# A layer norm's root and rows on GpSimd, and low parts by subtraction on VectorE, in a linear-attention and mixture-of-experts kernel

## The chip, the cores and the metric

One core of a Trainium2 chip runs the whole program. The metric is device microseconds (us) from start to end of one execution, as the median of several runs. The core has TensorE (matmuls; PE in the profile), VectorE (DVE), ScalarE (ACT), GpSimd (POOL) and SyncE (SP, which here only issues DMAs). GpSimd can't read the matmul banks (PSUM); the others can.

## The reference

```python
x = L0_attn_x                                    # (8, 512, 256), fp32
xn = (x - mean(x)) / sqrt(var(x) + 1e-5)         # over the last axis
out = x + attention(xn) + ffn(xn)

# attention: 16 heads of 16, 128 random features
q, k, v = split(xn @ W_qkv.T)
q_p = elu(q @ proj) + 1;  k_p = elu(k @ proj) + 1          # per head, 16 -> 128
kv = k_p.T @ v;  z = 1 / (q_p @ k_p.sum(tokens) + 1e-8)
attention = ((q_p @ kv) * z) @ W_out.T + b_out

# ffn: 8 experts, each token to its 2 best
logits = xn @ Wr + br; weights = softmax of the two largest logits, 0 elsewhere
ffn = sum over experts e of weights[:, e] * (gelu(xn @ W1[e] + b1[e]) @ W2[e] + b2[e])
```

## The kernel before

The program has two parts. The attention part works through 8 batches of 512 tokens and lasts until about 300 us; the expert part works through tiles of up to 384 tokens and is not touched by the change.

Matmuls run in fp32r, a rounded form of fp32. To keep fp32's accuracy, each operand is held as two parts: a high part (the value rounded to fp32r) and a low part (value minus high part, rounded). A product is then three matmuls (`mm3`, lines L527 to L529). The low part of queries, keys and head outputs is made in this way: ScalarE copies a PSUM bank into the high tile (`qk_hi`, L1038, into kdh or qdh; `at_hi`, L1067, into ath), TensorE multiplies that tile by the negated identity `minus` and adds it onto the same bank (`qk_rest`, L555; `heads_rest`, L647), so that the bank holds the low part, and ScalarE copies it out (`qk_lo`, L1043, into kdl or qdl; `at_lo`, L1071, into atl). For the tokens themselves (`tokens_lo`, L1395, into xTl) VectorE subtracts the high tile from the bank, one instruction of 128x512, and TensorE has no part in it.

A batch b is one call of `iteration(b)` on each of TensorE, ScalarE and VectorE, with 32 units u. Each unit makes the features of one bank: TensorE computes F (L590 in units 0 to 15, L596 in 16 to 31), ScalarE takes the exponential (`exp`, L1063, into a ring of four), VectorE combines both (`features`, L1468, into kp or qp). TensorE's unit u waits until VectorE has done the features of unit u - 4. Between the units, in an order written out by hand for each engine (`if u == ...`), lies the rest: attention of batch b - 1, and queries, keys, values, router and layer norm of the batches b + 1 and b + 2. Order within an engine is strict; semaphores tie the engines together, also where a bank is used again. In the order of TensorE: `tokens_T` of the next batch in unit 2 (it needs xn), `kv` in units 10, 11, 17 and 19 (L605), `qk_rest` of bank 0 in unit 11, of bank 1 in unit 18, of bank 2 in unit 23 and of bank 3 in unit 30, `to_heads` (L640) in units 20 and 27, which write banks that the low parts of keys and queries must have left, `heads_rest` in units 21 and 28, `state_T` (L613) at unit 26.

The layer norm of batch b + 2 is made on VectorE: `norm_stats` (4 instructions, L1350) in units 16 and 17, `norm_var` (4 small ones, L1355) in unit 18, nine small steps of 128x4 (`norm_step`, L1363 to L1379: variance plus eps, a bit-trick first guess of 1/sqrt, and two refinements) in units 19 to 29, and `norm_rows` (4 instructions of 128x256, L1386, which write xn) in unit 0 of the next iteration. `load_x` on SP refills xin once `norm_rows` has read it.

GpSimd, in each iteration b, scatters the 512 token rows to the experts' lists (`send`, 8 indirect DMAs, L1866, each waiting for a unit of TensorE: 0, 2, 4 to 14), adds the output bias to the residual (`add_bias`, L1853) and copies the next batch's xn into rows (`copy_rows`, L1860). SP issues the DMAs that stack the high and low parts into Sk and Sq (`stack_k`, `stack_q`, 12 DMAs each, L350), and the loads of x.

Of the kernel before, what the change touches and what calls it, by code (L numbers as in the profile page):

```python
# [19 lines left out]
I32 = mybir.dt.int32  # L20
# [33 lines left out]
C_END = C_OFF + E * TT  # L54


def constants():

    import numpy as np
    c = np.zeros((P, C_END), np.float32)  # L60
    p = np.arange(P)
    c[:, C_ID:C_ID + P] = np.eye(P)
    c[:, C_TRI:C_TRI + P] = p[:, None] < p[None, :]
    c[:, C_SLOT:C_SLOT + NT * E] = np.tile(np.arange(E) * CAP - SKIP, NT)
    c[:, C_TOK:C_TOK + NB * NT] = (NT * p[:, None, None] + NTOK * np.arange(NB)[:, None] + np.arange(NT)).reshape(P, -1)
    c[:, C_PAD:C_PAD + SUB] = p[:, None] + P * np.arange(SUB) + TOKENS
    c[:, C_EPS] = 1e-8 * DOWN * (p % 32 >= HD)
    c[:, C_T:C_T + TT] = np.arange(TT)
    c[:, C_LIM:C_LIM + E] = np.arange(E) * CAP - 2 * P
    c[:, C_OFF:C_OFF + E * TT] = (np.arange(E)[:, None] * CAP + T * np.arange(TT)).reshape(-1)  # L70
    return c


def build(nc, x, w_in, proj, w_out, b_out, experts, b1, b2, br, consts, out):
# [170 lines left out]
    xn_first = sem("xn_first")  # L245
    xT_full = sem("xT_full")
# [74 lines left out]
    NORM_STEPS, CUBE = 9, 0.375  # L321
    STEPS_AT = {19: (0, 1), 21: (2,), 23: (3, 4), 24: (5,), 25: (6,), 26: (7,), 29: (8,)}
# [48 lines left out]
    def _(sp):  # L371
# [66 lines left out]
        with sp.Fori(1, NB - 2) as b:  # L438
            load_x(b + 2)
            stack_k(b + 1)  # L440
            stack_q(b + 1)
            store_o(b - 1)
            load_xres(b)
        stack_k(NB - 1)
        stack_q(NB - 1)
        store_o(NB - 3)
        load_xres(NB - 2)
# [76 lines left out]
    def _(pe):  # L524
# [145 lines left out]
        def iteration(b, first=False):  # L670
# [4 lines left out]
            for u in range(32):  # L675
# [32 lines left out]
                if u == 11:  # L708
                    kv(b, 1)
                    qk_rest(b + 1, 0)  # L710
# [10 lines left out]
                if u == 18:  # L721
                    qk_rest(b + 1, 1)
# [291 lines left out]
    def _(act):  # L1014
# [25 lines left out]
        def qk_lo(b, i):  # L1040

            act.wait_ge(qkr_full, 4 * b + i + 1)
            A((kdl, qdl)[i // 2][:, i % 2, :], QK_BANK[i][:, :], ACT.Copy).then_inc(qkl_rdy, 1)  # L1043
# [25 lines left out]
        def at_lo(b, g):  # L1069
            act.wait_ge(atr_full, 2 * b + g + 1)  # L1070
            A(atl[:, g, :], AT_BANK[g][:, :], ACT.Copy).then_inc(atl_rdy, 1)  # L1071
# [27 lines left out]
        def iteration(b, first=False):  # L1099
            for u in range(32):  # L1100
# [15 lines left out]
                if u == 11:  # L1116
                    qk_lo(b + 1, 0)
                if u == 15:
                    qk_hi(b + 1, 1)
                if u == 19:  # L1120
                    qk_lo(b + 1, 1)
                    v_copy(b + 1, 0)
                if u == 20:
                    copy_kv(b)
                    if not first:
                        at_hi(b - 1, 0)
                    qk_hi(b + 1, 2)
                    if not first:
                        at_lo(b - 1, 0)
                if u == 22:  # L1130
                    qk_lo(b + 1, 2)
# [164 lines left out]
    def _(dve):  # L1296
# [61 lines left out]
        def norm_step(b, i):  # L1358
# [5 lines left out]
            elif i == 1:  # L1364
                link(V.tensor_scalar(seed.bitcast(I32), var[:, :].bitcast(I32), -0.5, float(0x5F3759DF), ALU.mult, ALU.add))
# [157 lines left out]
        def iteration(b, first=False, ahead=True):  # L1523
            for u in range(32):
                if u == 0 and not first:
                    norm_rows(b + 1, 0, 4)
# [18 lines left out]
                if ahead:  # L1545
                    if u == 16:
                        norm_stats(b + 2, 0, 2)
                    if u == 17:
                        norm_stats(b + 2, 2, 4)
                        join()  # L1550
                    if u == 18:
                        norm_var(b + 2)
                    for i in STEPS_AT.get(u, ()):
                        norm_step(b + 2, i)
# [172 lines left out]
        iteration(0, first=True)  # L1727
        batch_steps = chain[1] - before
        with dve.Fori(1, NB - 2) as b:
            chain[:] = before + b * batch_steps, 0  # L1730
            iteration(b)
# [103 lines left out]
    def _(pool):  # L1835
# [9 lines left out]
        pool.reg_mov(turn, 33)  # L1845
# [16 lines left out]
        def send(b):  # L1862
# [17 lines left out]
            for n in range(NT):  # L1880
                for r in range(2):
# [5 lines left out]
                    send_block(n, r, sent)  # L1887

        pool.wait_ge(qkh_rdy, 2)
        copy_rows(0)  # L1890
        send(0)
        copy_rows(1)
        with pool.Fori(1, NB - 1) as b:
            send(b)
            add_bias(b - 1)
            copy_rows(b + 1)
        def split_weights(c):
# [87 lines left out]
```

## Time and profile before

| | |
|---|---|
| time, median of 3 runs (lowest to highest) | 700.12 us (699.78 to 701.21) |
| the profiled execution's own time | 700.86 us |
| its span, first to last instruction | 698.7 us |
| busy: PE, DVE, ACT, POOL | 682.9, 504.1, 475.3, 227.9 us |
| mean granted TensorE clock | 0.996 of full speed |

The durations below come from the profiled execution. A row of the timeline reads: start in us from the span's start, duration in us, engine, line, operation, output<-inputs, shape, xN for N neighbours merged in one row; in square brackets the time the engine stood idle before the row, and what ended it. Because instructions of one engine overlap a little at their edges, the cost of one on its engine is the distance from its start to the start of the next, not its duration. A row of a stretch (A:B) gives its length and then, for PE, PEld, DVE, ACT and POOL, the busy time and the number of instructions, then the granted clock, the DMA engines' busy share and GB/s.

### The profile page before, as it was taken

Reading aid. Unit: us, or ns where it says so; the run is one execution under the profiler, and the core shown is the slowest. Engines: PE = TensorE matmul, PEld = TensorE weight load, DVE = VectorE, ACT = ScalarE, POOL = GpSimd, SP = SyncE. Lnnn points to the kernel's source line nnn. Section 1 sums busy time; section 2 is a strip of 40 time slices with the busy share of each in tenths; the row PEclk is TensorE's granted clock in tenths of the full one; section 3 lists DMA queues with packets and bytes.
Section 4 is the critical chain, followed back from the end, with each engine's and each line's share of the span. In section 5 each row is a group of like instructions: output and inputs, shape, how many; then the busy total and the mean of one; then the engine's idle time right before and its main releaser. Section 6 shows DMA issues by size and latency. Waiting matters only on the chain.

```text
span 698.7 us, 17362 instructions
## 1 busy us (share of the span) xinstructions
PE 682.9 (98%) x5503; PEld 603.3 (86%) x5504; DVE 504.1 (72%) x1246; ACT 475.3 (68%) x875; POOL 227.9 (33%) x169
## 2 busy tenths in 40 slices
PE   8899999999999998999999999999999999999996
PEld 4666777777777776589999999999999999999996
DVE  8798888888888878748577675556777545577544
ACT  5687969696969696776557775447775444577553
POOL 2053232323232324643232532225233222322422
PEclk9999999999999999999999999999999999999999
DMA  8856474747474647765455663336556333454531
GB/s 266 200 182 170 108 228 106 228 106 228 106 228 106 198 106 223 224 189 142 100 98 118 145 167 46 46 47 106 178 71 167 48 52 53 81 131 107 69 48 23
DMA packets 87205, 91.65 MB, mean 131 GB/s; under 512 B 60049, under 2 KB 73361, under 8 KB 84897
## 3 DMA queue, kind: packets, MB, share of 16 engines
q1 hardware_dynamic: 71426, 59.36, 33.9%
q0 software_dynamic: 13872, 18.75, 15.2%
q10 hardware_dynamic: 1872, 13.11, 5.1%
q8 instruction: 17, 0.28, 0.2%
q14 instruction: 18, 0.15, 0.1%
HBM read 39.32 MB, written 26.67 MB: 94 GB/s over the span
## 4 chain that ended last, share of the span: by engine, by line
PE 82%; DVE 6%; issue 4%; ACT 2%; POOL 2%; DMA 2%; SPq 1%; POOLq 0%; DVEq 0%
PE F L527 9%; PE F L528 9%; PE F L529 9%; PE WK L527 5%; PE F L596 5%; PE WK L529 4%; PE WK L528 4%; PE NUM L527 4%; PE NUM L529 4%; PE NUM L528 4%; PE DEN L605 4%; PE DEN L527 4%; PE DEN L529 4%; PE DEN L528 4%; PE F L590 3%
## 5 line engine op out<-in xcount | busy, mean ns | idle before, releaser
L1932 POOL DMA_INDIRECT out<-ysb,icur x75 | 121.0, 1613 | 270.6 <-DVE ysb L1763 241.0
L1218 ACT ACTIVATE h<-F,b1c 128x384 f32<-128x384 f32 x200 | 112.2, 575 | 140.0 <-PE F L529 131.2
L1740 DVE TENSOR_TENSOR hl<-h,hh 128x768 fp32r<-128x768 f32 x100 | 96.1, 962 | 111.6 <-ACT hh L1222 111.6
L1063 ACT ACTIVATE e_ring<-F 128x512 f32<-128x512 f32 x256 | 145.7, 621 | 38.5 <-PE F L590 35.0
L527 PE MATMUL F<-gxh,wh 128*128 128x384 f32 (+1 forms) x400 | 128.6, 321 | 0.4 <-DVE wl L1641 0.4
L528 PE MATMUL F<-gxl,wh 128*128 128x384 f32 (+1 forms) x400 | 128.0, 320 | 0.0
L529 PE MATMUL F<-gxh,wl 128*128 128x384 f32 (+1 forms) x400 | 128.0, 320 | 0.0
L1866 POOL DMA_INDIRECT xg<-rows,slots x64 | 63.2, 988 | 174.0 <-PE F L590 158.8
L1468 DVE SCALAR_TENSOR_TENSOR kp<-F,e_ring 128x512 f32<-128x512 f32 x128 | 82.7, 680 | 13.2 <-PE DEN L605 6.2
L1468 DVE SCALAR_TENSOR_TENSOR qp<-F,e_ring 128x512 f32<-128x512 f32 x128 | 85.2, 683 | 8.5 <-ACT e_ring L1063 7.0
L1222 ACT ACTIVATE hh<-h 128x768 fp32r<-128x768 f32 x100 | 84.6, 846 | 3.3
L527 PEld LDWEIGHTS F<-gxh,wh 128*128 128x128 f32 x400 | 75.6, 189 | 2.5 <-issue 2.5
L528 PEld LDWEIGHTS F<-gxl,wh 128*128 128x128 f32 x400 | 75.6, 189 | 0.0
L529 PEld LDWEIGHTS F<-gxh,wl 128*128 128x128 f32 x400 | 75.6, 189 | 0.0
L590 PEld LDWEIGHTS F<-stacked_proj,Sk 97*128 97x128 f32 x256 | 38.0, 192 | 26.0 <-issue 13.9
L527 PE MATMUL DEN<-wh,hh 128*128 128x256 f32 x200 | 56.7, 283 | 0.6 <-issue 0.6
L527 PE MATMUL NUM<-wh,hh 128*128 128x256 f32 x200 | 56.6, 283 | 0.2 <-DVE hl L1740 0.2
L528 PE MATMUL DEN<-wl,hh 128*128 128x256 f32 x200 | 56.6, 283 | 0.0
L529 PE MATMUL DEN<-wh,hl 128*128 128x256 f32 x200 | 56.6, 283 | 0.0
L529 PE MATMUL NUM<-wh,hl 128*128 128x256 f32 x200 | 56.5, 283 | 0.0
L528 PE MATMUL NUM<-wl,hh 128*128 128x256 f32 x200 | 56.5, 282 | 0.0
L596 PE MATMUL F<-Sq,stacked_proj 97*128 97x512 f32 x128 | 52.3, 450 | 0.3 <-DVE qp L1468 0.3
(261 smaller groups left out, 1552.6 us busy)
## 6 DMA issues: line engine op xcount, KB each, us to landing
wraw<-experts ACTq DMA_DIRECT2D x12, 1024.0 KB, 6.2
gblk<-xg SPq DMA_DIRECT2D x100, 96.0 KB
Sk<-kdh SPq DMA_DIRECT2D x64, 128.0 KB, 2.3
Sq<-qdh SPq DMA_DIRECT2D x64, 128.0 KB
xin<-x SPq DMA_DIRECT2D x8, 512.0 KB, 5.5
Sk<-kdl SPq DMA_DIRECT2D x32, 128.0 KB, 2.4
Sq<-qdl SPq DMA_DIRECT2D x32, 128.0 KB
xres<-x SPq DMA_DIRECT2D x8, 512.0 KB
```

The lines of the kernel that those rows point to most:

```text
L527: nc.tensor.matmul(dst, wh_, mh_, start=first, stop=False)
L528: nc.tensor.matmul(dst, wh_, ml_, start=False, stop=False)
L529: return nc.tensor.matmul(dst, wl_, mh_, start=False, stop=last)
L590: last = nc.tensor.matmul(F[u % 4][:, s * D:(s + 1) * D], Sk[0:SROWS, place_of(pr), n * P:(n + 1) * P], stacked_proj[0:SROWS, 2 * pr:2 * p ...
L596: last = nc.tensor.matmul(F[h % 4][:, :], stacked_proj[0:SROWS, h, :], Sq[0:SROWS, place_of(h // 2), :], start=True, stop=True)
L1063: A(e_ring[:, u % 4, :], F[u % 4][:, :], ACT.Exp, bias=EXP_BIAS, scale=1.0 / DOWN).then_inc(exp_done, 1)
L1218: A(h32[:, m, :], F[m % 4][:, 0:T], ACT.Gelu, bias=b1c[:, w, m:m + 1]).then_inc(gelu, 1)
L1222: A(hh[:, 2 * q:2 * q + 2, :], h32[:, 2 * q:2 * q + 2, :], ACT.Copy).then_inc(hh_rdy, 1)
L1468: V.scalar_tensor_tensor(dst, F[u % 4][:, :], DOWN, e_ring[:, u % 4, :], ALU.max, ALU.min).then_inc(feat, 1)
L1740: V.tensor_tensor(hl[:, 2 * q:2 * q + 2, :], h32[:, 2 * q:2 * q + 2, :], f32(hh[:, 2 * q:2 * q + 2, :]), ALU.subtract).then_inc(hl_rdy, 1)
L1866: pool.indirect_dma_start(xg, bass.IndirectOffsetOnAxis(slots[:, k:k + 1], 0), rows[:, n, :], None, bounds_check=last_row, oob_is_err=Fals ...
L1932: pool.indirect_dma_start(out, bass.IndirectOffsetOnAxis(icur[:, s, :], 0), ysb[:, s, :], None, bounds_check=last_token, compute_op=ALU.ad ...
```

## The change

- `norm_stats`, `norm_var` and the first two norm steps move from units 16 to 19 to units 0, 1 and 2 of `iteration(b)` for b from 2 on; iterations 0 and 1 have them in units 16 to 18 (`late=True`). Iteration 6 has none in either kernel.
- The other seven steps leave VectorE for batches 2 to 7. GpSimd does them as eleven instructions of 128x4 (`norm_root`), each waiting for the one before by a semaphore. They stand behind the third of the eight scatters (for b from 2 on), or behind all of them (b = 0), or behind the bias (b = 1).
- `norm_rows` of batches 2 to 7 leaves VectorE. GpSimd does it behind `add_bias` and `copy_rows`, some 13 units earlier than VectorE did.
- `qk_rest` of banks 0, 1 and 2 goes, in iterations 0 to 6, and `heads_rest` of bank 0 in iterations 1 to 6; with them go ScalarE's copies of the low parts. VectorE subtracts instead (`qk_low` in units 8, 17 and 24; in iteration 0 unit 12 for the first; `heads_low` in unit 21). Bank 3, head bank 1, and the whole start and final iteration stay as they were.
- On SP, `load_x` stands between `stack_k` and `stack_q` instead of ahead of both, one batch further ahead.

```diff
+        def qk_low(b, i):
+            dve.wait_ge(qkh_rdy, 4 * b + i + 1)
+            high, low = ((kdh, kdl), (qdh, qdl))[i // 2]
+            V.tensor_tensor(low[:, i % 2, :], QK_BANK[i][:, :], f32(high[:, i % 2, :]), ALU.subtract).then_inc(qkl_rdy, 1)
+        def heads_low(b):
+            dve.wait_ge(ath_rdy, 2 * b + 1)
+            V.tensor_tensor(atl[:, 0, :], AT_BANK[0][:, :], f32(ath[:, 0, :]), ALU.subtract).then_inc(atl_rdy, 1)
...
 # TensorE, iteration
                 if u == 11:
                     kv(b, 1)
-                    qk_rest(b + 1, 0)
-                if u == 18:
-                    qk_rest(b + 1, 1)
                 if u == 21:
-                    if not first:
-                        heads_rest(b - 1, 0)
                     v_logits(b + 1, 1)
                 if u == 23:
-                    qk_rest(b + 1, 2)
...
 # VectorE
-        def iteration(b, first=False, ahead=True):
+        def iteration(b, first=False, ahead=True, late=False):
             for u in range(32):
-                if u == 0 and not first:
-                    norm_rows(b + 1, 0, 4)
+                if ahead and u == (16 if late else 0):
+                    norm_stats(b + 2, 0, 2)
+                if ahead and u == (17 if late else 1):
+                    norm_stats(b + 2, 2, 4)
+                    join()
+                if ahead and u == (18 if late else 2):
+                    norm_var(b + 2)
+                    for i in range(SEED_STEPS):
+                        norm_step(b + 2, i)
...
+                if u == (12 if first else 8):
+                    qk_low(b + 1, 0)
+                if u == 17:
+                    qk_low(b + 1, 1)
+                if u == 21 and not first:
+                    heads_low(b - 1)
+                if u == 24:
+                    qk_low(b + 1, 2)
...
 # GpSimd
+        def norm_rows(b, i):
+            pool.wait_ge(root_step, ROOT_STEPS * i + 11)
+            pool.wait_ge(rows_rdy, b)
+            pool.wait_ge(xT_full, KT * b)
+            for n in range(NT):
+                last = nc.gpsimd.tensor_scalar(xn[:, n, :], xin[:, n, :], mv[:, n, 0:1], rs[:, 1, n:n + 1], ALU.subtract, ALU.mult)
+            last.then_inc(xn_rdy, 1)
...
         send(0)
+        norm_root(2, 0)
         copy_rows(1)
-        with pool.Fori(1, NB - 1) as b:
-            send(b)
+        norm_rows(2, 0)
+        send(1)
+        add_bias(0)
+        norm_root(3, 1)
+        copy_rows(2)
+        norm_rows(3, 1)
+        with pool.Fori(2, NB - 2) as b:
+            send(b, root=b)
             add_bias(b - 1)
             copy_rows(b + 1)
+            norm_rows(b + 2, b)
```

## Rows read from the trace of the kernel before

**Rows 1.** Busy time of two stretches: iterations 0 and 2.
```profile
22.40:57.44 35.04, 32.00 (x288) 22.16 (x286) 30.04 (x104) 27.32 (x60) 9.14 (x9) 0.95 0.67 182
92.47:127.51 35.04, 34.92 (x332) 26.44 (x328) 31.00 (x90) 28.66 (x61) 11.24 (x11) 1.00 0.61 166
```

**Rows 2.** Timeline of PE, iteration 2 and the start of iteration 3.
```profile
92.47 0.50 PE L590 MATMUL F<-stacked_proj,Sk 97*128 97x256 f32 x2
...
102.07 0.50 PE L555 MATMUL NUM<-kdh,minus 128*128 128x512 f32 x1
102.41 0.65 PE L590 MATMUL F<-stacked_proj,Sk 97*128 97x256 f32 x4
...
109.03 0.60 PE L640 MATMUL WK<-cst,at 128*128 128x128 f32 x4
...
112.57 0.40 PE L555 MATMUL WK<-qdh,minus 128*128 128x512 f32 x1
112.81 0.28 PE L527 MATMUL DEN<-WTh,xTh 128*128 128x264 f32 x1
...
113.54 1.02 PE L596 MATMUL F<-Sq,stacked_proj 97*128 97x512 f32 x3
114.39 0.60 PE L613 MATMUL WK<-cst,kv_sb 128*128 128x128 f32 x4
...
127.51 0.50 PE L590 MATMUL F<-stacked_proj,Sk 97*128 97x256 f32 x2
```

**Rows 3.** Groups by line, DVE, 92.47 to 127.51: busy us, mean ns | idle.
```profile
L1350 DVE BATCH_NORM_STATS2 stats<-xin 128x6 f32<-128x256 f32 x4 | 1.5, 414 | 0.0
L1386 DVE TENSOR_SCALAR xn<-xin,mv,rs 128x256 f32<-128x256 f32 x4 | 1.4, 407 | 0.0
L1395 DVE TENSOR_TENSOR xTl<-WK,xTh 128x512 fp32r<-128x512 f32 x1 | 0.7, 691 | 0.9 <-issue 0.9
L1371 DVE SCALAR_TENSOR_TENSOR rtmp<-rtmp 128x4 f32<-128x4 f32 x1 | 0.2, 162 | 0.0
```

**Rows 4.** Timeline of DVE, iteration 2: its three idle places and one feature.
```profile
94.08 0.69 DVE L1395 TENSOR_TENSOR xTl<-WK,xTh 128x512 fp32r<-128x512 f32 x1 [0.85 <-issue]
94.69 0.68 DVE L1395 TENSOR_TENSOR xTl<-NUM,xTh 128x512 fp32r<-128x512 f32 x1
...
100.77 0.69 DVE L1468 SCALAR_TENSOR_TENSOR kp<-F,e_ring 128x512 f32<-128x512 f32 x1 [0.86 <-PE DEN L605]
...
109.30 0.69 DVE L1468 SCALAR_TENSOR_TENSOR qp<-F,e_ring 128x512 f32<-128x512 f32 x1
...
112.72 1.29 DVE L1468 SCALAR_TENSOR_TENSOR qp<-F,e_ring 128x512 f32<-128x512 f32 x2 [0.30 <-ACT e_ring L1063]
```

**Rows 5.** Timeline of DVE, iteration 0.
```profile
34.78 3.07 DVE L1468 SCALAR_TENSOR_TENSOR kp<-F,e_ring 128x512 f32<-128x512 f32 x5
37.77 0.68 DVE L1344 TENSOR_TENSOR WOl<-wout,WOh 128x512 fp32r<-128x512 f32 x1
```

**Rows 6.** Timeline of POOL, iteration 2.
```profile
98.31 0.97 POOL L1866 DMA_INDIRECT xg<-rows,slots  x1 [2.20 <-PE F L590]
...
106.56 2.41 POOL L1853 TENSOR_TENSOR xres<-xres,bo_bc 128x1024 f32<-128x1024 f32 x1
108.88 1.06 POOL L1860 COPY rows<-xn 128x1024 f32<-128x1024 f32 x1
```

**Rows 7.** DMA issues, 92 to 128 us: KB each, us to landing.
```profile
xin<-x SPq DMA_DIRECT2D x1, 512.0 KB, 7.0
```

**Rows 8.** Timeline of the start: a POOL copy, a DVE instruction beside it.
```profile
14.54 2.29 DVE L1339 SCALAR_TENSOR_TENSOR stacked_proj<-praw,phi 33x2048 fp32r<-33x2048 f32 x1
15.04 2.69 POOL L1860 COPY rows<-xn 128x1024 f32<-128x1024 f32 x1 [12.96 <-ACT kdh L1038]
```

**Rows 9.** Groups by line, POOL, 0 to 3 us: the smallest with a shape.
```profile
L1849 POOL MEMSET rows<- 128x32 f32 x1 | 0.1, 123 | 0.0
```

**Rows 10.** Timeline of SP, iteration 2: the last four stacking DMAs of the keys.
```profile
111.52 2.50 SPq L350 DMA_DIRECT2D Sk<-kdl  x4
```

More of the change, by code:

```diff
@@ L53 @@
 C_T, C_LIM, C_OFF = 324, 336, 344
-C_END = C_OFF + E * TT
+C_ROOT = C_OFF + E * TT
+C_END = C_ROOT + 4
+CUBE = 0.375
 def constants():
@@ L245, in build @@
     xn_first = sem("xn_first")
+    seed_rdy = sem("seed_rdy")
+    root_step = sem("root_step")
+    root_rdy = sem("root_rdy")
     xT_full = sem("xT_full")
@@ L437, in _ @@
         stack_q(1)
-        with sp.Fori(1, NB - 2) as b:
-            load_x(b + 2)
+        load_x(3)
+        with sp.Fori(1, NB - 3) as b:
+            stack_k(b + 1)
+            load_x(b + 3)
+            stack_q(b + 1)
+            store_o(b - 1)
+            load_xres(b)
+        for b in (NB - 3, NB - 2):
             stack_k(b + 1)
@@ L1040, in qk_lo @@
         def qk_lo(b, i):
-            act.wait_ge(qkr_full, 4 * b + i + 1)
+            act.wait_ge(qkr_full, i + 1 if isinstance(b, int) and b == 0 else 4 + b)
             A((kdl, qdl)[i // 2][:, i % 2, :], QK_BANK[i][:, :], ACT.Copy).then_inc(qkl_rdy, 1)
@@ L1364, in norm_step @@
             elif i == 1:
-                link(V.tensor_scalar(seed.bitcast(I32), var[:, :].bitcast(I32), -0.5, float(0x5F3759DF), ALU.mult, ALU.add))
+                guess = V.tensor_scalar(seed.bitcast(I32), var[:, :].bitcast(I32), -0.5, float(0x5F3759DF), ALU.mult, ALU.add)
+                if isinstance(b, int) and b < 2:
+                    link(guess)
+                else:
+                    guess.then_inc(seed_rdy, 1)
             elif i == 2:
@@ L1726, in _ @@
         before = chain[1] + ROUTE_STEPS
-        iteration(0, first=True)
+        iteration(0, first=True, late=True)
         batch_steps = chain[1] - before
-        with dve.Fori(1, NB - 2) as b:
+        iteration(1, late=True)
+        with dve.Fori(2, NB - 2) as b:
             chain[:] = before + b * batch_steps, 0
@@ L1860, in copy_rows, with norm_root, constant @@
             nc.gpsimd.tensor_copy(rows[:, :, 0:D], xn[:, :, :]).then_inc(rows_rdy, 1)
-        def send(b):
+        def norm_root(b, i):
+            G = nc.gpsimd
+            seed, cubic, root = rs[:, 1, :], rs[:, 0, :], rs[:, 1, :]
+            def constant(k):
+                return cst[:, C_ROOT + k:C_ROOT + k + 1].to_broadcast([P, NT])
+            pool.wait_ge(seed_rdy, i + 1)
+            G.tensor_tensor(rtmp[:, 0, :], seed, seed, ALU.mult).then_inc(root_step, 1)
+            pool.wait_ge(root_step, ROOT_STEPS * i + 1)
+            G.tensor_tensor(rtmp[:, 1, :], rtmp[:, 0, :], var[:, :], ALU.mult).then_inc(root_step, 1)
+            pool.wait_ge(root_step, ROOT_STEPS * i + 2)
+            G.tensor_tensor(rtmp[:, 0, :], rtmp[:, 1, :], constant(0), ALU.add).then_inc(root_step, 1)
+            pool.wait_ge(root_step, ROOT_STEPS * i + 3)
+            G.tensor_tensor(rtmp[:, 0, :], rtmp[:, 0, :], rtmp[:, 1, :], ALU.mult).then_inc(root_step, 1)
+            pool.wait_ge(root_step, ROOT_STEPS * i + 4)
+            G.tensor_tensor(rtmp[:, 0, :], rtmp[:, 0, :], constant(1), ALU.add).then_inc(root_step, 1)
+            pool.wait_ge(root_step, ROOT_STEPS * i + 5)
+            G.tensor_tensor(cubic, rtmp[:, 0, :], seed, ALU.mult).then_inc(root_step, 1)
+            pool.wait_ge(root_step, ROOT_STEPS * i + 6)
+            G.tensor_tensor(rtmp[:, 0, :], cubic, cubic, ALU.mult).then_inc(root_step, 1)
+            pool.wait_ge(root_step, ROOT_STEPS * i + 7)
+            G.tensor_tensor(rtmp[:, 1, :], rtmp[:, 0, :], var[:, :], ALU.mult).then_inc(root_step, 1)
+            pool.wait_ge(root_step, ROOT_STEPS * i + 8)
+            G.tensor_tensor(rtmp[:, 0, :], rtmp[:, 1, :], constant(2), ALU.mult).then_inc(root_step, 1)
+            pool.wait_ge(root_step, ROOT_STEPS * i + 9)
+            G.tensor_tensor(rtmp[:, 0, :], rtmp[:, 0, :], constant(3), ALU.add).then_inc(root_step, 1)
+            pool.wait_ge(root_step, ROOT_STEPS * i + 10)
+            G.tensor_tensor(root, rtmp[:, 0, :], cubic, ALU.mult).then_inc(root_step, 1)
@@ L1887, in send @@
                     send_block(n, r, sent)
+                    if root is not None and (n, r) == (1, 0):
+                        norm_root(b + 2, root)
         pool.wait_ge(qkh_rdy, 2)
```

35 lines of the change are left out of this document (10 added, 25 removed).

## The prediction

> **What bounds the kernel now.** I read the busy time by stretches first, because a share over the whole span says nothing of one stage. In iteration 2 TensorE is busy 34.92 of 35.04 us, VectorE 31.00, ScalarE 28.66, GpSimd 11.24, at the full clock [rows 1]. A busy TensorE can still be held up a little, so the second view is its timeline: unit 2 starts at 92.47 and again at 127.51, a period of 35.04 us [rows 2], and the starts within it follow each other at the pace of the moving columns (0.24 us for 512) nearly everywhere. Iterations 1 to 6 have that period. TensorE is the bound, and VectorE is next, with 4.0 us of air per iteration. Its own timeline tells where the air is: 0.85 us before it takes low parts of the tokens, 0.86 us in unit 8 (it waits for a `kv` to free kp), 0.30 us in unit 21, and smaller bits at the end [rows 4]. Between units 9 and 21 it has next to none. Iteration 0 is different: TensorE is busy only 32.00 of 35.04 us, VectorE 30.04 [rows 1], and from 34.78 on VectorE's features follow one another without a gap, 0.60 us each [rows 5]; there VectorE leads.
>
> **What TensorE loses.** One removed matmul costs the distance to the next start: 112.57 to 112.81, 0.24 us; 102.07 to 102.41 is 0.34, but 0.10 of it is the price of following a `kv`, which the next matmul will pay instead [rows 2]. Three in each of iterations 0 to 6 and one more in each of 1 to 6 are 27 matmuls, 27 x 0.233 = 6.3 us, or 0.93 per full iteration (0.233 is the finer value of the same distance). All lie on the engine that sets the pace, if the others follow.
>
> **What VectorE gains and loses.** A low part of 128x512 from a bank costs 94.69 - 94.08 = 0.61 us [rows 4]. Four are 2.44 us. It loses `norm_rows`, four of 407 ns that overlap to 1.3 us, and seven steps of about 162 ns [rows 3], 1.1 us with their gaps. So a full iteration's work stays within 0.1 us of what it was: 31.0 of now 34.1 us. Only the place of each can hurt.
>
> **Iterations 2 to 6, in place.** Units 0 and 1: four `norm_stats` (414 ns each [rows 3], 1.3 us) stand where `norm_rows` stood. Unit 2: `norm_var` and two steps, six small instructions, at most 6 x 0.16 = 0.97, with overlap some 0.7 us, in the 0.85 us of air ahead of 94.08 [rows 4]. Unit 8: `qk_low` of bank 0, 0.61 us in the 0.86 us ahead of 100.77 [rows 4]; without this cover it would delay features 8 and on, and TensorE with them. Units 16 to 26: 1.3 us of statistics, 0.7 us of `norm_var` with two steps and five other steps (0.8 us) go, three low parts (1.83 us) come, so VectorE comes out 1.0 us ahead, against the 0.93 us by which TensorE wants to be early. This is tight in one place: the three units from 113.54 on take 0.85 us until 114.39 instead of 3 x 0.233 plus 0.10, for the third needs the features that end at 112.72 + 1.29 = 114.01 [rows 2, 4]. They depend on the exponential of unit 22, which TensorE starts 0.70 us earlier, and on one that ScalarE no longer holds up by copies. `to_heads` in unit 20 writes the bank that the second low part must leave: TensorE comes there at 109.03 - 0.47 = 108.56 [rows 2]; VectorE, free of statistics, is through with that low part at about 108.2. I take 0.07 us per iteration as lost to such brushes: 5 x (0.93 - 0.07) = -4.3 us.
>
> **Iteration 1.** Here the statistics, `norm_var` and two steps stay in units 16 to 18, and what VectorE saves lies in unit 0, ahead of a wait for TensorE at unit 8, so it is no help later. The second low part comes where the feature of 109.30 begins (a batch earlier, 74.26): 0.24 us earlier by the removed matmul and the exponentials behind it, so it ends at 109.30 - 0.24 + 0.61 = 109.67, and `to_heads`, now at 109.03, starts 0.64 us late [rows 2, 4]. Then `heads_low` adds 0.61 more on VectorE, one step goes (-0.15), its 0.30 us of air is used up, and the features that TensorE needs at 114.01 end some 0.4 us later than now. After that TensorE works without a gap. Iteration 1: +0.4 instead of -0.93.
>
> **Iteration 0.** The first low part stands in unit 12, behind features 9 to 11 of the gapless stretch of [rows 5]: +0.61; the second in unit 17: +1.22; of the steps only 0.45 us are gone by unit 22, and the third low part comes in unit 24. TensorE has little slack there: with four banks in the ring, and features 0.60 us apart, unit 17 can't start before feature 13 ends, and the row of five, features 9 to 13, ends at 34.78 + 3.07 = 37.85, 0.1 us ahead of unit 17's start at 37.97. I find the features that unit 26 needs 0.6 to 0.7 us later than now, with nothing behind it to make that up. Iteration 0: +0.6 instead of -0.70.
>
> **GpSimd.** It has 35.0 - 11.2 = 23.8 us free. No trace row shows one of its 128x4 instructions. From below: the 128x32 memset of 123 ns [rows 9], and a wait on the one before, put at nothing: 11 x 0.123 = 1.4 us. From above: the 128x1024 copy of 1.06 us [rows 6], 11.7 us. I take 2.5 us, 0.1 more for each than the smallest row, for the wait. They begin after the third scatter (98.31 - 2.20 = 96.1) and end by 98.7; the fourth scatter was to start at 98.31, and 2.20 us of idle stand before it [rows 6]. So the scatters end when they did, and the bias (2.41) and the copy too: 109.9. `norm_rows` of 4 x 256 elements lies between a copy of 1024 (1.06) and a two-input instruction of 1024 (2.41) [rows 6]; I take 1.7. xn is ready at 111.6, while TensorE asks for it at 127.5. The Trainium skill, GPSIMD Engine Reference, 4.1, calls one-input work on GpSimd about as fast as VectorE; by that page it would be an estimated 1.1 us, and the sum the same.
>
> **SP.** `load_x` now waits behind the last stacking DMA, issued until 111.52 + 2.50 = 114.0 [rows 10], so xn is not what it waits for. It takes 7.0 us to land [rows 7]: 121. VectorE reads it from 125.6 - 0.9 on. Air: 3.7 us. What it no longer stands ahead of (the keys' stacking) can only come sooner. Iteration 1 is closer: its seeds come in unit 18, 77.4 with the delays above; then root 2.5, copy 1.06, rows 1.7: 82.7, landing 89.7, and the statistics of iteration 2 are due at 90.6 + 1.0 = 91.6. With 11.7 us for a root they would be 7 us late.
>
> **A shared port.** A GpSimd copy that takes 1.06 us elsewhere took 2.69 at 15.04, beside a VectorE instruction with both inputs in SBUF; it ended at 17.73, 0.90 us behind that one's end at 16.83 [rows 6, 8]. The Trainium skill, SBUF — State Buffer, Who interferes with whom, has the rule: VectorE with two SBUF inputs and a reading GpSimd instruction exclude one another for a whole instruction, and one that reads a bank and one tile does not. By that rule the trace agrees. Here the low parts read a bank, so they are free. Only VectorE's small router instructions read two tiles, and in iteration 1 `norm_rows` falls on them (82 us): up to 1.7 us on VectorE, with 2 us of TensorE's slack there; I put 0 in the sum and 1 us in the range.
>
> **Sum.** -4.3 + 0.4 + 0.6 = -3.3 us on the profiled execution's 700.86 (span 698.7, 2.16 us around it): 697.6. The runs' median of 700.12 lies 0.74 lower than that execution: **696.8 us**. The final iteration, start and expert part move along unchanged.
>
> **Rivals.**
> - *TensorE pays in full.* VectorE keeps up in iterations 0 and 1 too: -6.3, 693.8 us. For it: TensorE's waits are single tenths. Against: the gapless features. Chance 0.13.
> - *VectorE becomes the pace in all iterations.* If a low part hits a place without air each time (0.61 twice ahead of unit 26, as in iteration 1), each full iteration gives nothing: 5 x 0 + 1.0 = +1.0, 701.1 us; half of that, 699. Against: the removed 1.3 us of statistics in just that stretch. Chance 0.15.
> - *GpSimd is late.* From a root of about 10 us on, x lands after VectorE asks for it. Statistics sit ahead of features 0 and 1, so TensorE stops. If each of the 11 cost as much as a scatter, 0.97 us [rows 6] and a gap of some 0.3, the root were 14.2 us: some 4.2 us late in iterations 3 to 5, and 9 in iteration 2: +21.6, 718 us. Decides at 0.9 us per instruction, and between 0.4 and 0.9 only iteration 2 suffers (1 to 4 us, so 698 to 701). Against: 123 ns for a memset. Chance 0.07 for late in all, 0.05 for iteration 2 alone.
> - My forecast with its own range of 695.6 to 698.4: 0.60.
>
> **Range and chances.** Below, the first rival (0.13) is left out all but its near side; above, the late GpSimd. 694.6 to 700.4. A difference under 0.2% (1.4 us) can't be told from none. Faster: 0.60 + 0.13 + a few of the others = 0.75. Same: 0.15. Slower: 0.10.
>
> **What the profile after would show.** Right: 21 matmuls of L555 and 6 of L647 fewer, the period from unit 2 to unit 2 34.1 to 34.2 us in iterations 2 to 6 but 35 or more in 0 and 1, idle of TensorE in iteration 1 in front of `to_heads` released by VectorE's kdl, xTl still preceded by air, the root's instructions on GpSimd 0.2 to 0.3 us apart, and xn done before 113. Wrong: 34.1 also in iteration 1; a wait for x on VectorE in unit 0; features, not matmuls, ending TensorE's waits in iterations 2 to 6; GpSimd instructions of 128x4 near 1 us.

## The result, and the profile after

The changed kernel takes 695.18 us (median of 4 runs, 694.57 to 695.41), the kernel before, measured beside it, 700.07 (4 runs, 699.78 to 701.21). The ratio is 0.9924, with a 95% interval of 0.9912 to 0.9936: faster by 0.76%, where 0.47% (696.8 us) was forecast. The profiled execution took 695.41 us, its span is 693.6.

The head of the page first: the span, then busy time and number of instructions by engine.

```profile
span 693.6 us, 17240 instructions
PE 675.2 (97%) x5476; PEld 596.9 (86%) x5477; DVE 507.4 (73%) x1207; ACT 464.2 (67%) x848; POOL 270.4 (39%) x259
```

TensorE has 27 matmuls fewer (5503 before, 5476 now) and its busy time fell by 7.7 us. Some 2 us of that are not the matmuls' (before's profiled execution had a stretch at half clock, and the changed kernel with such a stretch is busy 677.3 us, see iteration 0 below). The span fell by 5.1. GpSimd is busy 42 us more, and under 0.3 us of that shows in the time.

Busy time by stretches, of iterations 1 and 2, from unit 0 to unit 0 (the columns are those of [rows 1]):

```profile
53.60:89.86 36.26, 34.31 (x328) 25.72 (x324) 32.60 (x90) 27.68 (x59) 20.56 (x27) 1.00 0.59 155
89.86:123.82 33.96, 33.84 (x328) 25.72 (x324) 31.40 (x84) 26.92 (x57) 18.42 (x25) 1.00 0.64 172
```

In iteration 2 TensorE is idle for 0.12 us of 33.96: it is still the bound, and the period has shrunk with its work. In iteration 1 it is idle for 1.95 us, and the period of 36.26 is longer than before. The unit-0 starts of both kernels (the first matmul of the unit on TensorE's timeline) give the time of each iteration:

| us | start of unit 0 | it. 0 | it. 1 | it. 2 to 5, each | it. 6 |
|---|---|---|---|---|---|
| before | 20.58 | 33.42 | 35.61 | 35.03 | 35.01 |
| after | 20.54 | 33.06 | 36.26 | 33.97 | 34.07 |
| difference | -0.04 | -0.36 | +0.65 | -1.07 | -0.94 |

The differences add up to -4.96 us, and what follows iteration 6 is 0.15 us shorter. So the gain comes from iterations 2 to 6 alone (-5.2 us), and iteration 1 takes 0.65 back.

The prediction counts from unit 2 to unit 2. By that count iteration 0 takes 33.85 us before and 33.78 after, iteration 1 35.03 and 35.40: +0.37. ([rows 1] begin iteration 0 at 22.40, but its unit 2 starts at 23.60, so the prediction's 35.04 for iteration 0 is 1.2 us too long.) The other 0.28 us of the +0.65 lie in units 0 and 1 of iteration 1.

**Units 0 and 1 of iteration 1.** TensorE's timeline, before and then after, has a wait for the last feature of iteration 0, and it grew from 0.51 to 0.78 us:

```profile
56.45 1.06 PE L623 MATMUL DEN<-qp,st_w 128*32 128x512 f32 x8 [0.51 <-DVE qp L1468]
```

```profile
56.32 1.06 PE L631 MATMUL DEN<-qp,st_w 128*32 128x512 f32 x8 [0.78 <-DVE qp L1479]
```

Ahead of that feature VectorE makes the slot numbers, in small instructions: from the first of them to the feature it takes 1.05 us before (54.66 to 55.71) and 1.33 after (54.26 to 55.59). Two of them on VectorE's timeline, before and then after:

```profile
55.04 0.19 DVE L1442 TENSOR_TENSOR rows<-exm,erec 128x32 f32<-128x32 f32 x1
...
55.51 0.14 DVE L1449 COPY rows<-cst 128x4 f32<-128x4 f32 x1
```

```profile
54.66 0.46 DVE L1453 TENSOR_TENSOR rows<-exm,erec 128x32 f32<-128x32 f32 x1
...
55.39 0.39 DVE L1460 COPY rows<-cst 128x4 f32<-128x4 f32 x1
```

GpSimd's `norm_rows` runs beside them, from 50.89 to 55.75. In the runs below the stretch takes 1.23 us (the changed kernel again), 1.32 (norm alone) and 1.17 (hybrid) where `norm_rows` lies over it, 1.05 with the low parts alone, which has no `norm_rows` on GpSimd, and 1.04 to 1.05 in the kernels with it in which it is through by then (norm alone and hybrid in the first job, three in the third). So this part of iteration 1's loss comes from GpSimd.

**Iteration 1.** TensorE's timeline has the wait that the prediction named; the bracket holds the idle time ahead and what ended it:

```profile
74.63 0.66 PE L648 MATMUL WK<-cst,at 128*128 128x128 f32 x4 [0.89 <-DVE kdl L1401]
```

And VectorE's timeline has its reason: two statistics stand ahead of the low part of the keys, and the bank comes free only behind it.

```profile
73.11 0.74 DVE L1346 BATCH_NORM_STATS2 stats<-xin 128x6 f32<-128x256 f32 x2
73.89 0.69 DVE L1401 TENSOR_TENSOR kdl<-WK,kdh 128x512 fp32r<-128x512 f32 x1
```

**Unit 26 of iteration 3**: TensorE's timeline, after and then before (the same place, one iteration later than in [rows 2]):

```profile
146.82 1.12 PE L604 MATMUL F<-Sq,stacked_proj 97*128 97x512 f32 x3
147.77 0.60 PE L621 MATMUL WK<-cst,kv_sb 128*128 128x128 f32 x4
148.13 0.48 PE L604 MATMUL F<-Sq,stacked_proj 97*128 97x512 f32 x1
```

```profile
148.58 1.02 PE L596 MATMUL F<-Sq,stacked_proj 97*128 97x512 f32 x3
149.44 0.60 PE L613 MATMUL WK<-cst,kv_sb 128*128 128x128 f32 x4
149.99 0.50 PE L596 MATMUL F<-Sq,stacked_proj 97*128 97x512 f32 x1
```

The three units ahead of `state_T` took 0.86 us (in iteration 2 0.85, [rows 2]) and now take 0.95, which is the brush that was forecast. But the one behind `state_T`, which came 0.55 us after it, now comes after 0.36: a wait of 0.19 us is gone, which the prediction hadn't in its sum.

**GpSimd, iteration 2.** Timeline of POOL; between its first and last row of root lie nine more of 0.20 us, 0.28 apart:

```profile
96.36 0.23 POOL L1887 TENSOR_TENSOR rtmp<-rs 128x4 f32<-128x4 f32 x1
...
99.17 0.20 POOL L1907 TENSOR_TENSOR rs<-rtmp,rs 128x4 f32<-128x4 f32 x1
99.91 1.01 POOL L1922 DMA_INDIRECT xg<-rows,slots  x1 [0.55 <-issue]
...
108.82 1.05 POOL L1877 COPY rows<-xn 128x1024 f32<-128x1024 f32 x1
110.18 4.84 POOL L1915 TENSOR_SCALAR xn<-xin,mv,rs 128x256 f32<-128x256 f32 x4 [0.31 <-POOL rows L1877]
```

The root takes 99.37 - 96.36 = 3.0 us, and the copy starts at 108.82, 0.06 earlier than in [rows 6]. `norm_rows` takes 4.84 us, where 1.7 was taken and 2.41 was the upper bound: xn is ready at 115.02, long before TensorE asks for it in unit 2 of iteration 3 (126.68), but later than the 113 that the prediction named. SP's timeline and then the landing (DMA issues, 105 to 125 us: KB, us to landing) show what waits for it:

```profile
111.46 2.50 SPq L356 DMA_DIRECT2D Sk<-kdl  x4
115.20 0.35 SPq L394 DMA_DIRECT2D xin<-x  x1
```

```profile
xin<-x SPq DMA_DIRECT2D x1, 512.0 KB, 3.4
```

The stacking is issued by 113.96; `load_x` goes out at 115.20, 0.18 us behind the end of `norm_rows`. It lands in 3.4 us and not in the 7.0 of [rows 7], at 118.6, and VectorE reads x 6 us later.

### The profile page after: what moved, and what is told of

Same layout as the page of the kernel before. It is cut to its first block, busy times and chain, and to the rows that moved or that the text cites. A ratio compares the mean times of both kernels' runs of the same rounds, so it can differ in the third digit from the quotient of the medians.

```text
span 693.6 us, 17240 instructions
## 1 busy us (share of the span) xinstructions
PE 675.2 (97%) x5476; PEld 596.9 (86%) x5477; DVE 507.4 (73%) x1207; ACT 464.2 (67%) x848; POOL 270.4 (39%) x259
## 4 chain that ended last, share of the span: by engine, by line
PE 81%; DVE 9%; issue 3%; ACT 2%; DMA 2%; SPq 1%; POOLq 0%; DVEq 0%; POOL 0%; ACTq 0%
PE F L535 9%; PE F L537 9%; PE F L536 9%; PE WK L535 5%; PE WK L537 4%; PE WK L536 4%; PE F L604 4%; PE NUM L536 4%; PE NUM L537 4%; PE NUM L535 4%; PE DEN L613 4%; PE DEN L535 4%; PE DEN L536 3%; PE DEN L537 3%; DVE kp L1479 3%
## 5 line engine op out<-in xcount | busy, mean ns | idle before, releaser
L1065 ACT ACTIVATE e_ring<-F 128x512 f32<-128x512 f32 x256 | 143.6, 610 | 46.8 <-PE F L598 42.2
L1479 DVE SCALAR_TENSOR_TENSOR qp<-F,e_ring 128x512 f32<-128x512 f32 x128 | 82.4, 681 | 5.0 <-ACT e_ring L1065 4.8
```

The lines of the kernel that those rows point to most:

```text
L1065: A(e_ring[:, u % 4, :], F[u % 4][:, :], ACT.Exp, bias=EXP_BIAS, scale=1.0 / DOWN).then_inc(exp_done, 1)
L1479: V.scalar_tensor_tensor(dst, F[u % 4][:, :], DOWN, e_ring[:, u % 4, :], ALU.max, ALU.min).then_inc(feat, 1)
```

## The experiments

Twelve runs in three jobs (a job is a set of kernels measured side by side with the kernel before). In the first and the third job every kernel, the one before too, took some 20 us more than in the second, with stops of TensorE between its `kv` matmuls that the profiles of before, after and the second job don't have; so only ratios within a job are compared, and the second job, in which the kernel before took 700.52 us (17 runs), carries the readings.

**The low parts alone.** The kernel before, with `qk_low` and `heads_low` on VectorE in place of TensorE's and ScalarE's parts; root, rows and statistics stay where they were.

```diff
 # before, TensorE's and ScalarE's order: taken out
-                    qk_rest(b + 1, 0)     # and (b + 1, 1), (b + 1, 2), heads_rest(b - 1, 0)
-                    qk_lo(b + 1, 0)       # and (b + 1, 1), (b + 1, 2), at_lo(b - 1, 0)
 # VectorE's order: put in
+                if u == (12 if first else 8):
+                    qk_low(b + 1, 0)
+                if u == 17:
+                    qk_low(b + 1, 1)
+                if u == 21 and not first:
+                    heads_low(b - 1)
+                if u == 24:
+                    qk_low(b + 1, 2)
```

> The low parts alone are moved to VectorE; the whole norm stays there as before. Theory A (VectorE sets the pace in any iteration in which statistics and steps share units 16 to 26 with the low parts, and TensorE's removed matmuls are worth nothing there): iterations 1 to 5 get longer, by 0.6 to 1.2 us each, as iteration 1 of the changed kernel did (+0.65); iteration 6, without statistics, gains 0.9; iteration 0 loses 0.6. Time 702.5 to 706, slower than before. Theory B (27 matmuls of 0.233 us count wherever they lie): 693.8.

Measured: a ratio of 1.0048 [1.0035, 1.0061].

The same kernel in the second job:

> Low parts moved, norm left on VectorE. Theory A: slower than before by 2 to 6 us, iterations 1 to 5 longer than before's by 0.4 to 1.2 us each, iteration 6 shorter by 0.9. Theory B: 6.3 us faster.

Measured: 704.13 us (703.66 to 705.15), ratio 1.0049 [1.0036, 1.0062], so +3.6 us, and the same in both jobs. Its periods are 33.78, 36.35, four of 35.60, and 34.03. Its busy time in iteration 3:

```profile
126.52:162.12 35.60, 34.35 (x329) 25.66 (x325) 32.94 (x95) 27.17 (x57) 11.24 (x10) 1.00 0.60 164
```

TensorE is idle for 1.25 us. Its timeline in iteration 3 shows where, and VectorE's timeline why:

```profile
146.71 0.66 PE L640 MATMUL WK<-cst,at 128*128 128x128 f32 x4 [0.97 <-DVE kdl L1388]
```

```profile
145.10 0.74 DVE L1337 BATCH_NORM_STATS2 stats<-xin 128x6 f32<-128x256 f32 x2
145.97 0.69 DVE L1388 TENSOR_TENSOR kdl<-WK,kdh 128x512 fp32r<-128x512 f32 x1
```

That is the wait of iteration 1 of the changed kernel, here in every iteration that has statistics in units 16 to 19. Iteration 6 has none there, and its period is 34.03, 0.98 below that of before. That it is the place of the statistics, and not the rest of the norm's work on VectorE, is seen in the changed kernel: its iteration 1 has only the statistics, `norm_var` and two steps late, and takes 35.40 us from unit 2 to unit 2 where its next ones take 33.96. That is 1.44 of the 1.63 us by which the iterations here are longer than the changed kernel's. Theory A was borne out. Taking four matmuls from the engine that sets the pace made the kernel slower.

**The norm alone.** The changed kernel, with the low parts back on TensorE and ScalarE; root, rows and the next tokens on GpSimd, statistics in units 0 to 2.

```diff
 # after, TensorE's and ScalarE's order: put back
+                    qk_rest(b + 1, 0)     # and the others of the diff above
+                    qk_lo(b + 1, 0)
 # VectorE's order: taken out
-                if u == (12 if first else 8):
-                    qk_low(b + 1, 0)      # and the other three calls
```

> The norm alone is moved (statistics in units 0 to 2, root and rows on GpSimd); low parts on TensorE and ScalarE as before. Theory A: TensorE has as many matmuls as before and only its waits of 0.1 to 0.3 us per iteration for features can go: period 34.9 in iterations 2 to 6, time 698.9 to 699.6. Rival (the norm's move is itself worth half of the gain): 697.6 or less. Another (GpSimd's instructions hold VectorE's): 700.5 or more.

Measured: 1.0004 [0.9994, 1.0014].

> Norm moved, low parts left on TensorE. Theory A: only the waits of 0.1 to 0.3 us per iteration in units 26 and 27 go: 0.5 to 1.5 us faster than before. Rival: 2.5 us or more faster. The other: 0.5 us or more slower.

Measured: 699.77 us (698.98 to 700.66), ratio 0.9987 [0.9978, 0.9996], so -0.75 us of 700.52. Its periods are 32.98, 35.85, and five of 35.00. The busy time of iteration 3:

```profile
124.07:159.07 35.00, 34.89 (x333) 26.43 (x329) 29.32 (x80) 28.62 (x61) 18.43 (x25) 1.00 0.61 167
```

VectorE has 5.7 us of air here, where it had 4.0, and TensorE doesn't use it: the period is 35.00 us, where 34.9 was expected. Iteration 1 is 0.24 us longer than before's although it has all its old matmuls; that is the wait in its units 0 and 1. The wait behind `state_T` is still there, on TensorE's timeline (148.83 to 149.36 is 0.53 us):

```profile
148.83 0.60 PE L621 MATMUL WK<-cst,kv_sb 128*128 128x128 f32 x4
149.36 0.50 PE L604 MATMUL F<-Sq,stacked_proj 97*128 97x512 f32 x1
```

So the norm's move alone doesn't remove it. ScalarE's timelines show what else is needed. The norm alone:

```profile
146.51 1.10 ACT L1071 ACTIVATE e_ring<-F 128x512 f32<-128x512 f32 x2
147.46 0.63 ACT L1051 ACTIVATE qdl<-WK 128x512 fp32r<-128x512 f32 x1
147.94 0.64 ACT L1071 ACTIVATE e_ring<-F 128x512 f32<-128x512 f32 x1
```

The changed kernel:

```profile
145.34 1.80 ACT L1065 ACTIVATE e_ring<-F 128x512 f32<-128x512 f32 x3
147.02 0.18 ACT L1052 ACTIVATE lraw<-NUM 128x8 f32<-128x8 f32 x1
```

With the low parts on ScalarE, the copy of qdl stands between two and a third exponential; without it all three follow each other. But that alone isn't enough either. With the low parts alone moved, the three exponentials follow each other too (149.29 to 151.10 in iteration 3), and TensorE still waits behind `state_T`, on its timeline 0.56 us:

```profile
151.87 0.60 PE L613 MATMUL WK<-cst,kv_sb 128*128 128x128 f32 x4
152.43 0.50 PE L596 MATMUL F<-Sq,stacked_proj 97*128 97x512 f32 x1
```

There VectorE is late, with statistics, steps and low parts ahead of its features; in iteration 6, which has no statistics and no steps, the distance is 0.36. In iteration 1 of the changed kernel, with the statistics late but no steps behind unit 18, it is 0.36 too. So the 0.19 us come only where ScalarE's copy and VectorE's norm work around unit 26 are both gone; the runs don't separate that work further.

**The changed kernel again**, in the second job:

> The changed kernel, unchanged, for a ratio on the same chip as the next three. 0.993 of before where the kernel before takes 700 us. On a chip on which TensorE is held up in its dense kv stretches besides (the kernel before took 720 us there), less: the removed matmuls lie beside such stalls.

Measured: 696.25 us (694.93 to 697.17), ratio 0.9931 [0.9919, 0.9944], so -4.3 us. The parts are +3.6 and -0.75; their sum, +2.9, has the other sign. The two don't add: the norm's move is worth little by itself, and nearly 8 us once the low parts want the place of the statistics.

This job also answers what the run of the kernel before was to tell (its own run, below, has too many stops for it). Of the kernel before's 17 runs, eight have a mean granted clock of 0.995 to 0.997 and took 701.01 to 701.91 us, nine have 0.998 to 1.000 and took 699.54 to 700.52; the profiled executions with 0.996 have the stretch at half clock, those with more don't. So it comes and goes with the execution, and costs 1.3 us by the medians. The changed kernel had 0.996 in five of its six runs, so the -4.3 sets mostly low-clock runs against a mixture. Like against like it is 5.0 us faster (696.38 against 701.36), and the sixth run, at 0.999, 5.2 (694.93 against 700.09). The parts are then +2.9 and +3.7 (low parts), -0.9 and -0.5 (norm).

**A hybrid.** The changed kernel, but with TensorE's and ScalarE's low parts kept in iterations 0 and 1, where nothing was to be gained.

```diff
-        iteration(0, first=True)
-        with pe.Fori(1, NB - 1) as b:
+        iteration(0, first=True, rests=True)      # rests: qk_rest, heads_rest, qk_lo, at_lo as before
+        iteration(1, rests=True)
+        with pe.Fori(2, NB - 1) as b:
 # VectorE
-                if u == (12 if first else 8):
+                if u == 8 and not late:           # late: iterations 0 and 1; so too for the other three
```

> Norm as in the changed kernel, but low parts by VectorE only from iteration 2 on; iterations 0 and 1 have TensorE's seven matmuls back. Theory A: VectorE no longer holds TensorE in iterations 0 and 1, which take what they took before or a little less, and 2 to 6 keep 33.97: 694.0, 1.2 us under the changed kernel. Theory B: seven matmuls are paid again: 695.2 + 1.6 = 696.8.

Measured: 720.37 us (717.81 to 724.62), ratio 0.9997 [0.9981, 1.0013]. The run of the kernel before under its own label:

> The kernel before, unchanged. Its profiled execution had TensorE at half clock for 3.4 us from 27.0 us on, the changed kernel's had not; that is worth 1.0 us between 26.7 and 29.1 us. If the low clock belongs to the kernel, each run here shows a mean clock of 0.996 and 700.1 us. If it comes by chance, some runs show 0.998 and a time 1 us lower, and the profile here may be without it.

Measured: 720.25, ratio 0.9995 [0.9986, 1.0004]. It says how little two runs of one kernel differ in this job. TensorE's timeline in it has the stops:

```profile
112.09 0.27 PE L605 MATMUL DEN<-kp,vext 128*32 128x128 f32 x1 [0.19 <-issue]
112.79 0.86 PE L605 MATMUL DEN<-kp,vext 128*32 128x128 f32 x20 [0.43 <-issue]
```

Nothing that the trace shows is waited for ("issue"), in the midst of a `kv`. The hybrid in the second job:

> Low parts by VectorE only from iteration 2 on, norm as changed. Theory A (VectorE sets the pace in iterations 0 and 1): 0.998 of the changed kernel's time on the same chip, 1.2 us less. Theory B (matmuls count wherever they lie): 1.6 us more.

Measured: 696.02 us (695.21 to 696.6), ratio 0.9928 [0.9916, 0.9941]. Its iterations 0 and 1 take 32.68 + 35.80 = 68.48 us, 0.84 less than the 69.32 of the changed kernel; the norm alone, with the same work there, takes 68.83, 0.49 less. So in these profiles the low parts cost 0.5 to 0.8 us there. In the hybrid's execution unit 0 of iteration 0 began 0.47 us later, though, and the ratios of the two kernels can't be told apart; at like clock the hybrid isn't faster (695.45 against 694.93, and 696.51 against 696.38). Neither the 1.2 us less of Theory A nor the 1.6 us more of Theory B was measured.

**WOl earlier.** In iteration 0 the low part of the output weights (0.61 us of VectorE) stands in unit 14; here in unit 8, where VectorE has air.

```diff
-                if u == 14 and first:
-                    weights_out_lo()
                 if first and u == 8:
                     numbers_of(0)
+                    weights_out_lo()
```

> The changed kernel, with one instruction of VectorE (the low part of the output weights, 0.61 us) moved in iteration 0 from unit 14, in the gapless stretch, to unit 8, where VectorE stands idle for 1.04 us until a kv is done. Theory A (VectorE's gapless stretch sets the pace of iteration 0): iteration 0 from 33.1 (or 33.7 with the low clock) to 32.5 (33.1), 0.6 us less in all. Theory B (TensorE sets it): no change.

Measured: 718.52 us against 721.35, ratio 0.9973 [0.9955, 0.9991].

> The same move, in the kernel that leaves the low parts of iterations 0 and 1 to TensorE. Theory A: VectorE has less to do there, so little more comes of it: 0 to 0.4 us under that kernel, 0.990 to 0.993 of before. Theory B: no change against it.

Measured: 721.54, ratio 1.0002 [0.9983, 1.0021], where 0.990 to 0.993 was expected. Both ran in the third job, where the stops in iteration 0 are larger than the 0.6 us in question, and the changed kernel itself is not in it. The question is not settled.

**GpSimd's root made three and five times as long.** Ahead of the root stand 22, then 44 more 128x4 instructions, each with its wait; their result is not used.

```diff
+            for again in range(IDLE_STEPS):
+                G.tensor_tensor(rtmp[:, 0, :], seed, seed, ALU.mult).then_inc(root_step, 1)
+                pool.wait_ge(root_step, ROOT_STEPS * i + again + 1)
```

> The changed kernel; GpSimd's root has 22 more instructions (its first one again and again, 0.28 us each, 6.2 us more). Theory A (its work has 2.4 us of air in iteration 1 and about 6 in the others, 3.3 us after landing): x for iteration 2 lands about 3.5 us late, VectorE waits for it in unit 0 once; no wait in iterations 3 to 5. 2.5 to 3.5 us more than the changed kernel, 698 to 699. Rival (GpSimd's instructions hold up VectorE's through the shared port all along): longer periods in every iteration.

Measured: 738.45 us, ratio 1.0244 [1.0228, 1.026].

> The same with 44 more instructions, 12.3 us more, so that the root costs what the prediction's rival put on it. Theory A: x is late in iteration 2 by 9 us and in 3 to 5 by 4 to 6 us each: 712 to 720. If the air is larger than I think: under 705.

Measured: 742.53 us, ratio 1.0279 [1.0256, 1.0302].

VectorE's waits for x (us in all, times, longest), with three times the root and then with five times:

```profile
DVE stats L1346 <- DMA xin<-x: 4.3, 1, 4.3
```

```profile
DVE stats L1346 <- DMA xin<-x: 12.1, 2, 10.6
```

With three times the root x is late once, by 4.3 us, near the 3.5 expected. But the time is 17 us above the kernel before, and 20 above the same job's kernel with WOl earlier, where 2.5 to 3.5 was expected, and I had expected no longer periods from iteration 3 on: they are 41 us where WOl earlier has 36.5. The wait for x is not what does it. Nor is it the rival, VectorE held up by GpSimd all along: VectorE is busy 31.64 us here and 31.34 there. Iteration 3's busy time, three times the root:

```profile
142.84:183.98 41.14, 37.95 (x329) 28.23 (x325) 31.64 (x84) 26.90 (x57) 22.82 (x47) 0.92 0.50 142
```

and TensorE's timeline in it, then GpSimd's:

```profile
160.47 1.01 PE L613 MATMUL DEN<-kp,vext 128*32 128x128 f32 x18
161.80 0.39 PE L613 MATMUL DEN<-kp,vext 128*32 128x128 f32 x3 [0.33 <-issue]
...
164.75 0.41 PE L613 MATMUL DEN<-kp,vext 128*32 128x128 f32 x3 [1.04 <-issue]
166.20 0.59 PE L604 MATMUL F<-Sq,stacked_proj 97*128 97x512 f32 x1 [1.04 <-issue]
```

```profile
160.27 0.98 POOL L1925 DMA_INDIRECT xg<-rows,slots  x1 [0.30 <-issue]
```

The stops lie in `kv` matmuls over which the delayed scatters now run, and the granted clock falls to half behind them (0.92 over the iteration): of the 4.6 us, 2.6 are busy time of TensorE and 2.0 idle. That the scatters cause them is a coincidence in time and no more: 18 `kv` matmuls from 160.47 on run beside one of them without a stop, and no kernel without scatters was tried. With five times the root x is 10.6 us late once and 1.5 us a second time, not in each of iterations 3 to 5 as expected: the longer periods (39 to 40 us) may give GpSimd the time back. So the test says that x can be late, and when; it gives no clean price for it.

## Why the prediction was right, and where its sizes were off

**TensorE's 27 matmuls, paid only where VectorE keeps up.** Right: 21 of one line and 6 of the other are gone, the steady period fell by a whole iteration's share, and iteration 1 grew. The rival by which TensorE pays in full (693.8) falls with iteration 1's +0.65. The rival by which VectorE sets the pace everywhere (701.1) is the low parts alone, 1.0049: its mechanism is real, and it is mostly the removal of the statistics from units 16 to 19 that keeps it out, as the sum said ("VectorE comes out 1.0 us ahead").

**Iterations 2 to 6: -0.86 forecast each, -1.07 and -0.94 measured.** The mis-sized step is "I take 0.07 us per iteration as lost to such brushes". Four matmuls gave 4 x 0.236 = 0.94; the brush at unit 26 cost 0.09; the wait behind `state_T` gave back 0.19. Together -1.04; iteration 6 gained 0.1 less, and why is open. I had counted ScalarE's freed copies only as a condition for the units to keep pace, and not looked for a wait of TensorE that ends once they and VectorE's norm work there are gone. This part of the sum was 0.9 us too cautious. [rows 2] end one row before the matmul behind `state_T`, where the wait is.

**Iteration 1: +0.4 forecast, +0.37 measured by the same count, from unit 2 to unit 2.** The place, the releaser and the size were right: `to_heads` was to start 0.64 us late and starts 0.75 late, counted from unit 2 (74.63 - 57.32 = 17.31 us against 109.03 - 92.47 = 16.56). The 0.65 of the table has 0.28 more, from GpSimd's `norm_rows` at the seam to iteration 0, a term that the sum had at 0 (see the shared port). The air before xTl, which was to stay, is gone as well:

```profile
94.32 0.69 DVE L1395 TENSOR_TENSOR xTl<-WK,xTh 128x512 fp32r<-128x512 f32 x1
```

There is no bracket: xTl is reached 4.46 us into the iteration, just as before (94.08 - 89.62), but with nothing to spare. I expect that one more instruction in units 0 to 2 would move TensorE; no run here shows it.

**Iteration 0: +0.6 forecast, -0.36 measured (-0.07 from unit 2 to unit 2).** Part of this difference isn't the change. Busy time from 26 to 31 us, before and then after (the last three columns are granted clock, DMA share, GB/s):

```profile
26.00:31.00 5.00, 4.90 (x26) 4.30 (x27) 3.62 (x16) 2.46 (x7) 0.00 (x0) 0.66 0.79 182
```

```profile
26.00:31.00 5.00, 4.67 (x32) 3.87 (x32) 4.19 (x18) 3.62 (x8) 0.00 (x0) 1.00 0.93 206
```

The clock of 0.66 is 3.4 us at 1.2 GHz and 1.6 at 2.4 (1.6 + 3.4 / 2 = 3.3 of 5). From 26.10 to 30.79 the kernel before does what the changed one does from 26.04 to 29.89: 0.84 us longer. Both had been idle for 1.54 us just ahead. The changed kernel run again has the same stretch (0.66), the norm alone and the hybrid haven't: it comes and goes with the execution. Both with it, iteration 0 takes, from unit 2 to unit 2, 34.35 us against 33.85: +0.50; with the 0.84 taken off before's, 33.78 against 33.01: +0.77. So the total was near +0.6. What makes it up was only half right, and that is luck: the norm alone and the hybrid, whose low parts in iteration 0 are before's, take 33.72 and 33.35. So 0.1 to 0.4 us are the low parts' (two executions with the same work there differ by 0.37; with the whole norm left on VectorE the low parts cost 0.51, 34.36 against 33.85), and the rest comes with the norm's move, 0.2 to 0.27 of it by `norm_rows`. The premise "35.04 us" and the sign "35 or more in 0" came from the wrong start of the stretch. VectorE's features stay gapless and the low parts push them, as the timeline of VectorE shows:

```profile
33.99 1.88 DVE L1479 SCALAR_TENSOR_TENSOR kp<-F,e_ring 128x512 f32<-128x512 f32 x3
35.78 0.68 DVE L1401 TENSOR_TENSOR kdl<-NUM,kdh 128x512 fp32r<-128x512 f32 x1
```

**GpSimd.** The root was well sized (2.5 forecast, 3.0 measured), `norm_rows` wasn't: "lies between a copy of 1024 and a two-input instruction of 1024" failed, 4.84 us. The estimate by the Trainium skill, GPSIMD Engine Reference, 4.1, of 1.1 us was further off. Its consequence failed too: xn is what `load_x` waits for. x was in time all the same, because the landing took 3.4 us and not 7.0. In iteration 1 the two nearly met: `load_x` goes out at 85.15 and lands after 3.2 us at 88.35, and VectorE asks for x at 90.82. With the 7.0 us that the prediction used it would have landed at 92.15, 1.3 us late. Two errors cancelled there.

**The shared port.** The 0 in the sum was wrong by 0.2 to 0.27 us, inside the 1 us put in the range, and at another place than feared. First the copy: VectorE's row in iteration 0, and GpSimd's copy beside it:

```profile
49.99 0.72 DVE L1421 TENSOR_TENSOR dlt<-lg,top 128x32 f32<-128x32 f32 x1
```

```profile
49.63 1.04 POOL L1877 COPY rows<-xn 128x1024 f32<-128x1024 f32 x1 [0.25 <-DMA xg<-rows,slots]
```

0.72 us instead of 0.19, and it ends at 50.71 behind the copy's 50.67. By the rule of the Trainium skill, SBUF — State Buffer, Who interferes with whom, the trace agrees here. TensorE stands idle no longer behind it than before (0.20 us in both kernels). Beside `norm_rows` in iteration 1 (80.12 to 84.98), where the prediction feared it, the same instruction keeps its time:

```profile
83.07 0.19 DVE L1421 TENSOR_TENSOR dlt<-lg,top 128x32 f32<-128x32 f32 x1
```

But beside `norm_rows` at the seam of iterations 0 and 1 the rows shown at the start are longer: the one with two inputs by 0.27 us, the copy of 128x4 by 0.25 (0.18 to 0.33 in the other profiles of the second job that have `norm_rows` there). TensorE waits for the feature behind them, by 0.27 us more than before, and 0.20 in the changed kernel run again. So beside GpSimd's `tensor_scalar` some small instructions of VectorE are held up and others not; none loses the 1.2 us of a whole `tensor_scalar`. What decides it is open.

**The sum.** On the profile's own account: iterations 2 to 6 gave 0.9 us more than forecast, iteration 0 1.0 more (most of it the half clock of before's execution), iteration 1 0.25 less. That makes 1.65 of -4.96 against -3.3. In the medians the gain is 4.9 us, and like clock against like clock 5.0 and 5.2 in the second job; the -4.3 there, nearer to the forecast, is a matter of the clock. The mis-sized step that is shown is the 0.07 us; it gives 0.9 of the 1.6 to 1.9 us, and the rest of the medians' difference is not placed.

## What to carry to other kernels

Work taken from the engine that sets the pace pays only where the engine that takes it over has air at that very place in the order: the same matmuls gave +0.5% with the norm left on VectorE and -0.7% with it moved, and most of that difference is whether statistics stood in front of one low part. So test the parts of such a change together, and cost each by the stretch of order it lands in, not by busy time. When a copy leaves an engine, look through the bound engine's timeline for every start that waited behind that copy, for that is gain too. And compare profiles at the same granted clock: here a stretch at half clock, which comes and goes, is worth a quarter of the effect.

## What the runs showed of the hardware

- GpSimd's `tensor_scalar` with two scalars per partition took 1.22 us for 128x256, more than its copy of 128x1024 (1.05); VectorE took 0.41 for the same. Groups by line of POOL, after:

```profile
L1915 POOL TENSOR_SCALAR xn<-xin,mv,rs 128x256 f32<-128x256 f32 x24 | 29.1, 1217 | 1.7 <-POOL rows L1877 1.7
```

- GpSimd's 128x4 instructions took 0.20 us, and 0.28 from start to start with a wait on the one before.
- Beside that `tensor_scalar` small VectorE instructions took up to 0.33 us more in some places (0.39 and 0.47 instead of 0.14 for a copy of 128x4), and nothing more in others.
- A landing of 512 KB took 7.0 us when issued 1.7 us behind a store and 1.1 behind a load of the same size, 3.2 to 3.4 when issued behind the stacking.
- TensorE fell to half clock for 3.4 us in some executions and not in others of the same kernel, after the same 1.54 us of idle. Runs with the lower mean clock took 1.3 us more.
- In two of three jobs TensorE stopped inside `kv` for 0.2 to 1.4 us with nothing recorded that it waited for. The cause is open, and so is whether scatters beside it matter.
